# Packed causal attentions: step 1's maxima moved behind the first scores, and inverted sums fetched ahead of maxima

## The reference, cut to what matters

```
attn = q @ k.T * scale
attn = where(causal, attn, -inf)
attn = softmax(attn, axis=-1)
y = attn @ v
```

## Time and profile before

| | us |
|---|---|
| median of 3 runs | 3255.83 |
| lowest and highest | 3252.84, 3267.48 |
| the profiled execution, span | 3262.6 |
| l0a: first item, first scores, step 1's scores | 148.0, 182.7, 196.0 |
| l1a: first item, first scores, step 1's scores | 1145.5, 1162.7, 1169.6 |
| l3a: first item, first scores, step 1's scores | 2560.6, 2589.5, 2599.9 |

### The profile page before, as it was taken

The page is one execution under the profiler, slowest core; times in us unless marked ns, Lnnn a source line. Parts: engine busy times, 40 slices in busy tenths (PEclk is TensorE's granted clock), DMA queues, the critical chain, the costliest instruction groups (busy, mean ns, idle before and its releaser), DMA issues. The chain is left out here.

```text
span 3262.6 us, 45065 instructions
## 1 busy us (share of the span) xinstructions
PE 2508.7 (77%) x15890; PEld 1399.0 (43%) x15890; DVE 1855.3 (57%) x5014; ACT 1480.5 (45%) x2984; POOL 996.1 (31%) x822
## 2 busy tenths in 40 slices
PE   6788885785667577888874669897776788859977
PEld 2323324564443233333352255564443333346666
DVE  6576655565645455555553558335432577656678
ACT  5334451453432156666641514224412355537876
POOL 1145561146347566666612300001101111101200
PEclk9889998897878789999986869997687799978989
DMA  3311101610444411111002210001000322114023
GB/s 112 94 43 42 42 2 36 229 54 19 125 154 101 108 47 46 35 41 46 17 15 67 34 39 1 10 4 30 14 1 33 74 28 28 16 48 123 1 78 104
DMA packets 186942, 174.52 MB, mean 53 GB/s; under 512 B 52777, under 2 KB 160042, under 8 KB 186462
## 3 DMA queue, kind: packets, MB, share of 16 engines
q1 hardware_dynamic: 172030, 153.84, 16.8%
q0 software_dynamic: 9408, 12.56, 2.5%
q10 hardware_dynamic: 5280, 5.24, 0.5%
HBM read 117.62 MB, written 57.40 MB: 54 GB/s over the span
## 5 line engine op out<-in xcount | busy, mean ns | idle before, releaser
L946 POOL TENSOR_TENSOR l1a_p_lo<-res,l1a_p_hi 128x1024 f16<-128x1024 f32 x192 | 311.9, 1643 | 177.2 <-ACT res L1187 177.2
L1196 ACT ACTIVATE l0a_probs<-ps 128x1024 f32<-128x1024 f32 (+1 forms) x192 | 145.5, 810 | 176.2 <-PE ps L1050 103.7
L1196 ACT ACTIVATE l3a_probs<-ps 128x1024 f32<-128x1024 f32 (+1 forms) x192 | 146.9, 809 | 143.3 <-PE ps L1050 116.2
L1186 ACT ACTIVATE l1a_p_hi<-ps 128x1024 f16<-128x1024 f32 x192 | 157.8, 822 | 110.9 <-PE ps L1050 82.8
L1047 PE MATMUL ps<-l1a_qs,l1a_ks 128*128 128x512 f16 (+3 forms) x768 | 167.7, 333 | 31.6 <-ACT res L1187 31.6
L1016 PE MATMUL ps<-l1a_ks,l1a_qs 128*128 128x512 f16 (+3 forms) x384 | 122.2, 347 | 78.7 <-DVE l1a_nmax L1221 33.0
L1218 DVE CUSTOM_DVE_ANT_0 l1a_masked<-ps,l1a_wide_mask 128x128 bf16<-128x128 f32 (+3 forms) x256 | 118.0, 490 | 103.1 <-PE ps L1016 100.9
L971 POOL TENSOR_TENSOR l0a_both<-l0a_probs 128x768 f32<-128x768 f32 (+2 forms) x96 | 154.7, 1633 | 46.3 <-PE ps L1088 46.0
L1187 ACT ACTIVATE res<-ps 128x1024 f32<-128x1024 f32 x192 | 158.1, 823 | 0.0
L1050 PE MATMUL ps<-mask_t,ident_b 128*128 128x128 bf16 x768 | 157.5, 225 | 0.0
L1218 DVE CUSTOM_DVE_ANT_0 l0a_masked<-ps,l0a_wide_mask 128x128 bf16<-128x128 f32 (+3 forms) x256 | 116.5, 489 | 68.0 <-PE ps L1016 67.3
(11 more groups left out here) (749 smaller groups left out, 6453.7 us busy)
## 6 DMA issues: line engine op xcount, KB each, us to landing
f_wf<-in_L_ffn_w_dram SPq DMA_DIRECT2D x16, 1024.0 KB
f_slots<-x0a_zeros SPq DMA_DIRECT2D x32, 256.0 KB, 3.4
f_xe<-f_slots SPq DMA_DIRECT2D x32, 256.0 KB, 3.0
f_ys<-f_y SPq DMA_DIRECT2D x32, 256.0 KB
l1a_qs<-l_q_h SPq DMA_DIRECT2D x64, 128.0 KB
d_wall<-in_L_ffn_W_dram SPq DMA_DIRECT2D x3, 2112.0 KB
l0a_qs<-l_q_h SPq DMA_DIRECT2D x32, 128.0 KB
l0a_ks<-l_k_h SPq DMA_DIRECT2D x16, 256.0 KB
```

The lines of the kernel that those rows point to most:

```text
L946: pool.tensor_tensor(ph_lo[:, n % SLOTS, :, 0:w], probs[:, n % FULL, :, 0:w], ph_hi[:, n % SLOTS, :, 0:w], ALU.subtract).then_inc(s_["low_ ...
L1186: act.activation(ph_hi[:, n % SLOTS, :, 0:w], SB[n % 2][:, :, 0:w], ACT.Exp)
L1196: act.activation(probs[0:KR, n % SLOTS, 2 * pr:2 * pr + 2, 0:w], SB[x % 2][:, :, 0:w], ACT.Exp).then_inc(s_["exps"], 1)
```

## The change

Three things are changed. In a causal plan only step 0's items stand in `before`. The items of later steps are taken from one list, and `ahead` says how far each step goes in it: step 0 takes all of step 1 and nothing of step 2; step 1 takes step 2 and three quarters of step 3; step 2 the rest of step 3 and 0.6 of step 4; step 3 the rest of step 4 and all of step 5; from then on the order is as before. Beside step 0 the items lie at units 0 to 2 only, since unit 3 comes after the scores of step 1's first unit. In SyncE's list the inverse row of step s-3 stands before the rows of step s.

```diff
-        before = [add(it) for s in range(self.lead) for it in self.maxima(s)]
+        if self.key_rows == P:
+            first, ahead = 1, {0: 0.0, 1: 0.75, 2: 0.6}
+        else:
+            first, ahead = self.lead, {}
+        before = [add(it) for s in range(first) for it in self.maxima(s)]
+        coming = [it for s in range(first, S) for it in self.maxima(s)]
         for s, st in enumerate(self.steps):
-            todo = self.maxima(s + self.lead) if s + self.lead < S else []
-            cost = [0.15 + st.firsts[0].w / 900 if it[0] == "max" else 0.7 for it in todo]
+            todo = []
+            last = s + self.lead
+            upto = int(ahead.get(s, 1.0) * len(self.maxima(last))) if last < S else 0
+            while coming and (coming[0][1] < last or coming[0][1] == last and upto > 0):
+                upto -= coming[0][1] == last
+                todo.append(coming.pop(0))
+            cost = [0.15 + self.steps[it[1]].firsts[0].w / 900 if it[0] == "max" else 0.7 for it in todo]
...
+            if ahead.get(s) == 0.0:
+                parts = [p for p in parts if p[0] < self.first_unit[s + 1] - 1]
...
                 for s in range(S):
                     if (split or paired) and s > LEAD:
                         sum_columns(s - LEAD - 1)
+                        inverse_row(s - LEAD - 1)
                     maximum_rows(s)
-                    if (split or paired) and s > LEAD:
-                        inverse_row(s - LEAD - 1)
```

## The result

| | before | after |
|---|---|---|
| median of 4 runs (of before one more than in the first table), us | 3254.34 | 3334.97 |
| lowest and highest, us | 3252.53, 3267.48 | 3333.53, 3343.14 |
| ratio, 95% interval | | 1.0243 [1.0225, 1.026] |
| the profiled execution, span, us | 3262.6 | 3333.1 |
| l0a: first scores, step 1's scores, us after the first item | 34.6, 48.0 | 25.3, 57.7 |

The kernel became slower, as forecast, but by 81 us and not by 31: 3335 lies beyond the upper end of the range, 3304. Times of a stage are counted from its first item from here on, since all later stages are shifted, and a step begins at its first scores. The three stages together hold +79.4 us in the profiled pair; the other stages ended 9 us shorter there, without any part of the change in them.

What follows compares the result with a forecast made beforehand. It took the preludes to go at the pace of VectorE and TensorE taking turns. Terms 23.9 + 8.2 - 2.5 + 1.5 = +31 us: profiled span about 3294, forecast 3287 against the median, range 3265 to 3304.

Steps and rivals of the forecast that it cites:

- net at step 1's scores: l0a, l1a, l3a: step 1's scores begin later by 3.7, 10.0 and 10.2 us, sum +23.9 (+19.2 to +32.0).
- First scores, and the wait in front of them: l0a, l1a, l3a: scores start 10.2, 0.2 and 4.5 us earlier, once step 0's rows land; VectorE idles behind TensorE's wait.
- Step 0: Lasts a lead-in, step 1's maxima (21.0, 10.8, 18.9 us in l0a, l1a, l3a) and 2.6 us for the rows.
- Later steps: Steps 1 to 3: lagging maxima cost 2.3 us in l0a, 1.4 in l1a, 4.5 in l3a; sum +8.2 (+4 to +12).
- Inverted sums first: SyncE's list in l0a: inverse rows go out earlier, 0.36 us in each of seven small steps, -2.5 (0 to -3.7).
- Clock: Each stage: TensorE nearly idle some 3 us in the new wait, its clock falls, +1.5 us (0 to +6).
- cold start rival: TensorE stays at 1.2 GHz through step 0 and falls back after the open wait: +43, 3299 us; chance 0.08.
- Hidden maxima: VectorE keeps up, each of 83 moved items costs 0.17 us: -3, 3253 us; chance 0.12, shared with early rows.
- the faster rival: Step 0's rows land 2.6 us after their turn, 26 us come off; with maxima hidden -29, 3227 us; chance 0.06.
- my pace: The forecast's own pace for the maxima; with step 0's rows landing early it gives +5, 3261 us.
- the change might not do what it says: The planner leaves step 1's maxima ahead, so only the swap on SyncE counts: 3253 us; chance 0.02.

Runs made afterwards that it cites:

- filling the wait: The changed kernel with the first 16 maxima of step 1 (22 in l3a) kept ahead of the first scores: 3305.2 us against 3258.5.
- The added maxima: The kernel before with the sums' columns ahead of the loads, eight maxima done twice at steps 3, 7 and 11 of each stage: 3277.3 us against 3232.3.

## Why the prediction was right in direction and wrong in size

| term | forecast, us | measured, us |
|---|---|---|
| first scores, l0a / l1a / l3a | -10.2 / -0.2 / -4.5 | -9.4 / 0.0 / -2.6 |
| net at step 1's scores | +3.7 / +10.0 / +10.2 | +9.7 / +10.5 / +10.8 |
| items that lag, steps 1 to 3 (l1a 1 to 4) | +2.3 / +1.4 / +4.5 | +11.1 / +11.4 / +7.1 |
| inverse row ahead of the rows | -2.5 | -3.8 in l0a |
| what stands behind the load | 0 | +23 |
| clock, by itself | +1.5 | not separable |
| sum | +31 | +81 |

The first two rows are the kernel after against before; the third and fourth are the changed kernel against the one before, both with the sums ahead of the loads; the fifth is the difference of the medians, 49.3 less 26.2. Together the second to fifth are 31.0 + 29.6 - 3.8 + 23 = 80. This checks only part of the account: since the fifth is a difference of medians, the sum comes out because the other three, 56.8 us, nearly make up the 53.4 by which the changed kernel stands above the one before, both with the sums ahead.

Two terms failed, by about as much each: the price of the items that lag, 8.2 us forecast and 29.6 measured, and what stands behind the load, put at nothing and measured at 23. The net at l0a's step 1, mostly the length of its step 0, adds 6.

*First scores, and the wait in front of them.* Right. The windows in which the DMA share faded gave the landing within 2 us in all three stages, and the loss of VectorE's work behind TensorE's wait is confirmed by filling the wait (30 us back) and by removing it (25 us back). One reading was loose: the prediction counted 2 us from the end of an issue and found the trace of l1a against it. From the start of the issue TensorE used the rows after 1.82 us there (1160.87 to 1162.69) and after 1.77 in l0a with the rows ahead of the loads (160.70 to 162.47), so these rows do not speak against about 2 us.

*Step 0.* Within 0.6 us in l1a and l3a, in l3a by luck in part: the first scores came 1.9 us later than forecast and the step was 1.2 shorter. In l0a the term was mis-sized. I took 21.0 us for the 33 items, with bounds of 18.7 and 24.9; from the first (176.97) to the turn (202.16) they took 25.2. The choice followed the prelude's pace, in which two banks and half speed were already contained, but not that TensorE would do units in between while two banks give VectorE no stock. l3a with two banks shows half of the difference between the two stages; the rest stays open.

*Later steps.* This step of the working failed. 0.17 us an item was a mean: 34 items against none, in a step which without them has room. The added items come on top of the 34, where that room is used up; measured there, one costs 0.51 us in l0a and l3a and 0.30 in l1a, where eight of them brought another 4.4 us once, in the next step. The number of items was wrong too: not 13 but all 17 of step 2's (in l1a 9, not 8) are carried along: 8 more than before in step 1, 2 in step 2, 7 in step 3 (in l1a 4, 1 and 4). 17 x 0.51 = 8.7 for l0a and l3a, against 11.1 and 7.1 measured; in l1a 9 x 0.30 + 4.4 = 7.1 against 11.4, where step 4 shows the same pair of stretched operations. The price is that of maxima 512 wide in a large step, and the lag carries narrower ones too; what makes up the other 2.4 us in l0a and 4.3 in l1a stays open.

*Inverted sums first.* The mechanism was right and the size too low: 0.75 us a step, all that the trace had offered (0.6 earlier, 0.66 of idle time). What I left out is on the same queue.

*What stands behind a step that moved.* The working had no term for this, and it cost 23 us. I counted that rows and a load stand behind the new wait in SyncE's list, and gave the rows over 9 us of cover. But step 3's rows lost their cover for another reason: their turn itself had moved into the course of step 2, and with it the load behind them, and behind the load the columns of the sums, for which VectorE waits in its own list before it goes on with maxima. I followed the rows to their user and not the two further entries. That the columns were late behind a load already in the kernel before, by 2.4 to 3.3 us in each of l1a's large steps with a load, stood in the same trace; a look at who waits for L906 would have shown it.

*Clock.* The granted clock stayed at 0.50 in 193.9 to 210.9 of l0a and fell again after the wait in step 3. That is the cold start rival's mechanism, in part; its 3299 was still 36 us short, since it, too, had no term for the sums and took the low price for a lagging item.

*The other rivals.* Hidden maxima is excluded by the price of 0.5 us and by step 0's length; the faster rival named the right place from which it decides (with the rows ahead of the loads the first scores come at 16.2 us in l0a, as it said: 164.2 less 148.0) and what that brings, 25 us of the 26 it counted; its sum with my pace, +5, was as far off as the forecast's (with the rows ahead +52 was measured), by the same two terms. That the change might not do what it says is excluded by the first timeline.

## What to carry to other kernels

If a step's data goes out on a queue in order, follow every entry behind it to the engine that waits for it, not only the entry that moved: transfers of 0.6 us behind loads of 5 us cost 23 of the 81 us here, and 26 in the kernel before, unseen. Price an added item by what the last ones cost in a step that is already full, not by the mean of all. And before work is moved behind a wait, ask which engine that work keeps busy: here VectorE was busy for 7.81 of the last 10 us in front of l0a's first scores, so its work there was not idle time that could be saved.

## What the runs showed of the hardware

In l1a three kinds of tiny VectorE operations between SBUF tiles, if they begin during a GpSimd subtraction, end only after it. Timeline of the kernel after, step 4:

```profile
1268.22 2.12 POOL L957 TENSOR_TENSOR l1a_p_lo<-res,l1a_p_hi 128x1024 f16<-128x1024 f32 x1 [1.75 <-ACT res L1198]
1268.32 2.04 DVE L1253 TENSOR_TENSOR l1a_y_col<-l1a_y_col 128x8 f32<-128x8 f32 x1
...
1270.83 1.64 POOL L957 TENSOR_TENSOR l1a_p_lo<-res,l1a_p_hi 128x768 f16<-128x768 f32 x1 [0.49 <-ACT res L1198]
1270.84 1.65 DVE L1260 SCALAR_TENSOR_TENSOR l1a_r_parts<-l1a_r_col,l1a_r_parts 128x8 f16<-128x8 f32 x1
...
1272.76 0.50 PE L1027 MATMUL ps<-l1a_ks,l1a_qs 128*128 128x384 f16 x1 [3.47 <-DVE l1a_nmax L1229]
```

The first of these takes 0.14 us in the experiment with the sums ahead (shown above) and the second 0.17 in most steps; here they take 2.04 and 1.65 us, and TensorE stands 3.5 us until VectorE has emptied a bank again. The added maxima brought the same two lengths in l1a, 2.04 and 1.65, in the small step behind a lengthened large one, which is where its 4.4 us lie. The Trainium skill, page "SBUF — State Buffer", section "SBUF: two separate sides", describes a port pair that VectorE and GpSimd share as a lock held for a whole instruction, for VectorE operations with two inputs in SBUF among others; these rows agree with it. In the traces of all thirteen kernels, 241 of the 243 TENSOR_TENSOR, TENSOR_SCALAR and SCALAR_TENSOR_TENSOR operations of the inverted sums that began during such a subtraction ended after it, by 0.02 us in those shown, and none of the 16 RECIPROCALs did: these took 0.20 us as elsewhere. Every large step of l1a that took 24.8 us or more, the stage's last step left aside, holds one such operation of 1.7 to 2.1 us. A list that lags by a few items so changes which operations meet, and that can cost more than the items.
